# Merging an attention block and the routed experts behind it into one program, with eight expert blocks taken from early counts

## The chip, the cores and the metric

The kernel runs on one core of a Trainium2 chip. A core has a matrix engine (TensorE, PE in the profile, with its weight loads as PEld), a vector engine (DVE), an activation engine (ScalarE, ACT), a general engine (GpSimd, POOL) and a queue engine that issues transfers (SyncE, SP). Each engine takes its instructions in order, and they wait for each other by semaphores. The metric is the device time of one execution in microseconds (us); lower is better.

## The reference

Two layers run one after the other over x of 16 batches x 256 tokens x 128 features in float32. Each adds attention, normalises, adds a mixture of experts, and normalises again. The change lies in the first layer:

```python
# attention: 16 heads of 64, half-causal mask
scores = einsum('bhqd,bhkd->bhqk', q / sqrt(64), k);  attn = softmax(where(allowed, scores, -inf))
x = layernorm(x + (attn @ v) @ Wo)
# routed experts: 8 experts of 512, each token goes to its top two
topv, topi = top_k(x @ router_w.T + router_b, 2);  gates = softmax(topv)
for e in range(8):
    h = silu(x @ gate_w[e].T) * (x @ up_w[e].T)
    out += (h @ down_w[e].T) * sum(gates * (topi == e))
x = layernorm(x + out)
```

The second layer has a latent attention with rotary positions and another mixture of experts with two shared ones.

## The kernel before

The program is a sequence of stages: `attention0`, `routed0`, `attention1`, `routed1`, `final1`. The first two are the matter here.

`attention0` goes over 16 batches (numbered 0 to 15). A batch has eight pairs of heads and is worked in four periods (`period(i, u, batch)`, u from 0 to 3) of two pairs each. In a period TensorE makes scores, the value product of earlier pairs (`values`), the projections of the pair after next (`project_qk`, `project_v`) and transposes of probabilities (`turn`). DVE takes the maxima (`maxima`), ScalarE the exponentials (`exps`) and two kinds of copies out of PSUM (`turned`, `outputs`). The queue order of each engine is written out by hand in `period`; after period 3 of batch 15 comes a tail in which TensorE, ScalarE and DVE finish the last pairs. `project_v` may not start before `outputs` has freed its PSUM bank (`pe.wait_ge(ot_done, s - 2)`).

Tokens are routed as the batches go by. Period 1 makes the layernorm of the batch before (`residual`), period 3 its router, and period 0 of the next batch its choice of two experts: `choices` writes a one-hot tile, GpSimd keeps running counts per expert (`running_counts`), TensorE turns these into ranks (`ranks`), DVE into row numbers (`slots`), and GpSimd scatters each token's row into the memory region of its experts (`scatter_rows`, tensor xs). For the last batch all of this stands in the tail, one step behind the other, with nothing else left to do. When its choice is known, `tables` on DVE works out for each of at most 39 blocks of 256 rows which expert it belongs to (`expert`, `w_at`) and where its rows start (`in_at`).

Then the block of engine programs ends with a barrier, GpSimd clears the semaphores, and a second barrier follows (`nc.clear_and_free_semaphores`, `nc.all_engine_barrier`). `routed0` handles the 39 blocks. For each, SyncE loads its rows, TensorE transposes them (`turn_input`), ScalarE and DVE split inputs and weights into a high and a low part (`input_high`, `input_low`, `weights_high`, `weights_low`), TensorE makes gate and up products in two halves (`gate_up(j, u, 0)` and `(j, u, 1)`, 12 matmuls each) and the down product of the block before (`down`), ScalarE applies Silu (`gate`), DVE multiplies (`product`), ScalarE copies the result (`output`), and GpSimd scatters it with two indirect transfers (`scatter`, tensor yt). The first block runs with nothing before it to overlap with; the further ones run as a software pipeline, most of them in a hardware loop of eight blocks a turn. Behind `routed0` stands a barrier without a semaphore clear.

Of the kernel before, what the change touches and what calls it, by code (L numbers as in the profile page):

```python
# [21 lines left out]
P = 128  # L22
# [28 lines left out]
XW = P + 4  # L51
# [6 lines left out]
TAB = NB + 1  # L58
NB1 = 2 * NT // BR + E0 - 1
# [49 lines left out]
def attention0(nc, ctx, g, d):  # L109
# [4 lines left out]
    def sem(name):  # L114
# [44 lines left out]
    rk = sb("rk", [P, QB * 2, E0])  # L159
# [6 lines left out]
    before = sb("before", [P, P], F32R)  # L166
    S = g.psum[:, 0:4, :]
# [3 lines left out]
    VO = g.psum[:, 7, :]  # L171

# [14 lines left out]
    lg_ps, lg_done, oh_done, cum_done, rank_ps, rk_done, idx_done, count_ps = (sem(n) for n in (  # L187
        "lg_ps", "lg_done", "oh_done", "cum_done", "rank_ps", "rk_done", "idx_done", "count_ps"))
    zeroed, scattered, kept, pool_cum = sem("zeroed"), sem("scattered"), sem("kept"), sem("pool_cum")
    may_scatter, named = sem("may_scatter"), sem("named")  # L190
    rl_done, scaled = sem("rl_done"), sem("scaled")
    CONSTS = 4
# [7 lines left out]
    def after(eng, signal, n):  # L200

        if not isinstance(n, int) or n > 0:
            eng.wait_ge(signal, n)

    with nc.Block(no_gpsimd_drain=True) as block:
        @block.sync
        def _(sp):
# [45 lines left out]
            sp.wait_ge(w_in, 2 * B * 16)  # L253

        @block.scalar
        def _(act):
# [39 lines left out]
            def routed_columns(n):  # L296
                act.wait_ge(ntr_ps, n)
                nc.scalar.activation(halves(xr_h), TC, ACT.Copy).then_inc(nt_act, 1)
                nc.scalar.activation(halves(xr), TC, ACT.Copy).then_inc(nt_act, 1)

            def routed_ranks(n, bank=QK):
                act.wait_ge(rank_ps, n)
                nc.scalar.activation(rk[:], bank[:, 0:QB * 2 * E0].rearrange("p (g e) -> p g e", e=E0), ACT.Copy).then_inc(rk_done, 1)
# [8 lines left out]
            def period(i, u, batch):  # L312
# [15 lines left out]
                if u == 0 and batch > 1:  # L328
                    routed_ranks(i - 1)
# [3 lines left out]
                exps(s + 1, hp + 1, 1)  # L333

# [18 lines left out]
        def _(pool):  # L353
# [99 lines left out]
            scatter_rows(1, idx_last, nrm_last)  # L453
            pool.wait_ge(scattered, B * SCATTERS)

        @block.vector
        def _(dve):
# [104 lines left out]
            def slots(n, at=idx):  # L562
                dve.wait_ge(rk_done, n)
                chain.done(nc.vector.tensor_tensor(ohr[:], oh[:].bitcast(F32), rk[:], ALU.mult))
# [3 lines left out]
            def tables():  # L568
                t = g.t0

                wide = lambda a: a.unsqueeze(1).to_broadcast([P, TAB, E0])
# [2233 lines left out]
```

## Time and profile before

| | us |
|---|---|
| median of 3 runs | 1362.91 |
| lowest and highest run | 1362.71, 1364.22 |
| profiled execution, its own time | 1361.32 |
| its span, first to last instruction | 1359.5 |
| TensorE busy in the span | 1255.3 |
| DVE, ScalarE, GpSimd busy | 973.7, 922.3, 614.7 |

The views give, for the profiled execution, the instructions of each engine in order of time (timeline), their sum by source line (groups), and busy time, granted TensorE clock and transfers by stretch (windows). A clock of 1.00 is 2.4 GHz, 0.50 is 1.2 GHz. Matmuls overlap, and their ends are modelled, so a matmul that shows 0.28 us may be followed by the next after 0.12. The bracket behind a row of the timeline is the idle time of its engine before it and what ended that.

### The profile page before, as it was taken

How to read it: one execution, taken by the hardware profiler on the slowest of the kernel's cores; microseconds unless marked ns; L12 is line 12 of the kernel's file. 1: busy time of each engine (PE TensorE's matmuls, PEld its weight loads, DVE VectorE, ACT ScalarE, POOL GpSimd, SP SyncE). 2: the span in 40 equal slices, each digit the busy share in tenths (PEclk: the TensorE clock that was granted, in tenths of full speed). 3: DMA queues.
4: the chain of work that ended last, by engine and by line, in shares of the span. 5: the costliest groups of instructions: out<-in, count | busy, mean ns of one | idle time of the engine just before them, and what ended most of it. 6: DMA issues, size and time to landing. Idle time of an engine off the chain costs nothing. (4 is left out here: it accounts for less than half of the span.)

```text
span 1359.5 us, 34492 instructions
## 1 busy us (share of the span) xinstructions
PE 1255.3 (92%) x10782; PEld 1074.1 (79%) x10783; DVE 973.7 (72%) x2954; ACT 922.3 (68%) x2433; POOL 614.7 (45%) x967
## 2 busy tenths in 40 slices
PE   6999999999999999399999489999999999779996
PEld 5888888888888888399999467777777776558885
DVE  6788888877888876466666478899898987363443
ACT  4777777776677776265555357787878786657863
POOL 3244444444444444233333434465556552335773
PEclk9999999999999999599999769999999999989998
DMA  7021202020202020111111350222024200203326
GB/s 264 21 69 52 88 30 91 27 91 27 91 27 91 27 88 25 48 52 56 55 54 43 112 175 10 80 89 87 24 87 151 72 17 13 90 21 114 108 75 196
DMA packets 56445, 99.82 MB, mean 73 GB/s; under 512 B 11184, under 2 KB 46384, under 8 KB 53744
## 3 DMA queue, kind: packets, MB, share of 16 engines
q1 hardware_dynamic: 45840, 78.58, 18.2%
q0 software_dynamic: 9088, 18.89, 4.1%
q10 hardware_dynamic: 1440, 1.39, 0.3%
q8 instruction: 40, 0.66, 0.2%
q14 instruction: 37, 0.30, 0.1%
HBM read 77.85 MB, written 62.06 MB: 103 GB/s over the span
## 5 line engine op out<-in xcount | busy, mean ns | idle before, releaser
L271 ACT ACTIVATE a_prob<-psum,a_nmx 128x128 f32<-128x128 f32 (+1 forms) x512 | 208.2, 424 | 79.6 <-DVE a_nmx L496 79.6
L412 POOL TENSOR_TENSOR a_prob<-a_prob,a_rl 128x128 f32<-128x128 f32 (+1 forms) x256 | 124.4, 508 | 241.3 <-DVE a_rl L500 240.8
L2270 DVE TENSOR_REDUCE a_nmx<-psum 128x2 f32<-128x512 f32 x256 | 170.0, 685 | 22.5 <-PE psum L1555 19.4
L278 ACT ACTIVATE a_probt<-psum 128x768 f32<-128x768 f32 x128 | 105.1, 821 | 71.7 <-PE psum L716 71.7
L943 POOL DMA_INDIRECT yt<-m_yrow,m_dest x78 | 74.6, 957 | 129.2 <-ACT m_yrow L1018 117.4
L1927 ACT ACTIVATE a_prob<-psum 128x1024 f32<-128x1024 f32 x128 | 127.3, 1024 | 7.1 <-PE psum L1585 6.9
L1555 PE MATMUL psum<-k_stk,a_q_stk 96*128 96x256 f32 x512 | 117.2, 323 | 11.9 <-DVE a_nmx L2270 7.9
L1555 PEld LDWEIGHTS psum<-k_stk,a_q_stk 96*128 96x128 f32 x512 | 79.2, 197 | 42.8 <-issue 18.5
L716 PE MATMUL psum<-ident,a_prob 128*128 128x128 f32 x768 | 106.0, 274 | 1.7 <-ACT a_probt L278 1.0
L271 ACT ACTIVATION_READ_ACCUMULATOR a_prob<-psum,a_nmx 128x1 f32 x512 | 107.5, 210 | 0.0
L485 DVE TENSOR_TENSOR a_qkt<-psum,a_bqk 128x512 f32<-128x512 f32 x128 | 88.2, 689 | 22.0 <-PE psum L102 21.6
L1048 DVE TENSOR_TENSOR m_hid<-m_act_out,psum 128x512 f32<-128x512 f32 x78 | 53.6, 687 | 63.1 <-PE psum L102 46.2
L100 PE MATMUL psum<-m_x_h,m_w_h 128*128 128x256 f32 x312 | 95.3, 305 | 0.0
L1151 POOL DMA_INDIRECT yt<-m_yrow,m_dest x78 | 75.5, 968 | 41.9 <-DVE m_yrow L1298 21.3
L100 PE MATMUL psum<-a_xt_h,a_wqk_h 128*128 128x256 f32 x256 | 81.7, 319 | 8.5 <-DVE a_xt_l L481 7.1
L102 PE MATMUL psum<-m_x_l,m_w_h 128*128 128x256 f32 x312 | 89.1, 285 | 0.0
L101 PE MATMUL psum<-m_x_h,m_w_l 128*128 128x256 f32 x312 | 89.0, 285 | 0.0
L716 PEld LDWEIGHTS psum<-ident,a_prob 128*128 128x128 f32 x768 | 85.7, 141 | 2.3 <-issue 1.5
L496 DVE TENSOR_REDUCE a_nmx<-psum 128x2 f32<-128x512 f32 x128 | 87.0, 680 | 0.0
L1585 PE MATMUL psum<-a_q_stk,k_stk 128*128 128x256 f32 x512 | 85.4, 290 | 0.2 <-DVE a_o L2285 0.2
L1912 ACT ACTIVATE k_stk<-psum,a_in_head 96x256 fp32r<-96x256 f32 x192 | 74.5, 467 | 9.8 <-PE psum L1549 9.7
L2126 POOL DMA_INDIRECT xs<-a_nrm,a_idx x60 | 61.7, 1028 | 42.7 <-DVE a_idx L2356 27.3
(368 smaller groups left out, 3855.3 us busy)
## 6 DMA issues: line engine op xcount, KB each, us to landing
xs<-in_fill SPq DMA_DIRECT2D x144, 264.0 KB, 4.2
m_xrow<-xs SPq DMA_DIRECT2D x78, 132.0 KB, 2.1
w<-in_w SPq DMA_DIRECT2D x16, 256.0 KB, 3.4
a_yin<-yt SPq DMA_DIRECT2D x16, 256.0 KB, 2.7
f_yin<-yt SPq DMA_DIRECT2D x7, 512.0 KB, 8.0
w<-in_wr SPq DMA_DIRECT2D x2, 1284.0 KB, 7.8
yt<-m_yrow,m_dest POOLq DMA_INDIRECT x156, 2.2
xs<-in_fill_idle SPq DMA_DIRECT2D x2, 1056.0 KB, 6.6
```

The lines of the kernel that those rows point to most:

```text
L100: nc.tensor.matmul(out, wh, xh, start=start, stop=False)
L101: nc.tensor.matmul(out, wl, xh, start=False, stop=False)
L102: return nc.tensor.matmul(out, wh, xl, start=False, stop=stop)
L271: last = nc.scalar.activation(prob[:, hp % 4, h, at], S[:, 2 * (hp % 2) + h, at], ACT.Exp, bias=nmx[:, hp % 4, q, h:h + 1], accum_out=lsum ...
L278: nc.scalar.activation(probt[:, hp % 2], PT[:, :, 0:SW], ACT.Copy).then_inc(pt_done, 1)
L412: last = nc.gpsimd.tensor_tensor(prob[:, hp % 4, 0, at], prob[:, hp % 4, 0, at], rl[:, hp % 4, 0, q:q + 1].to_broadcast(prob[:, hp % 4, 0, ...
L485: nc.vector.tensor_tensor(qkt[:, hp % 2], QK.rearrange("p (j t) -> p j t", j=2), bqk[:, hp, :].unsqueeze(2).to_broadcast([P, 2, T]), ALU.a ...
L496: nc.vector.reduce_max(nmx[:, hp % 4, 1, :], two[:, :, P:SW], AX.X, negate=True).then_inc(nmx_done, 1)
L716: last = nc.tensor.transpose(PT[:, h, k * P:(k + 1) * P], prob[:, hp % 4, h, k * P:(k + 1) * P], g.ident[:])
L1555: last = nc.tensor.matmul(bank[:, q * T:(q + 1) * T], q_stk[0:KR, p, h // HG, q * P:(q + 1) * P], k_stk[p][0:KR, h, :], start=True, stop=True)
L1927: nc.scalar.activation(prob[:, k % 2, 2 * (t % 2):2 * (t % 2) + 2, :], ST[:, 2 * (t % 2):2 * (t % 2) + 2, :], ACT.Exp, scale=SCALE).then_i ...
L2270: nc.vector.reduce_max(nmx[:, :, h:h + 1], bank.rearrange("p (q k) -> p q k", q=QB), AX.X, negate=True).then_inc(mx_done, 1)
```

## The change

`attention0` and `routed0` become one function, `attention0_routed0`, in one block of engine programs with one set of semaphores. Of the 39 blocks, the first eight (`EARLY_BLOCKS`) are chosen differently: after 14 batches each expert has some full blocks of 256 rows, which later tokens can't change any more. The first eight of these are taken, in the order of the experts. Their table is worked out inside the last batch: `full_blocks` and `blocks_before` at the end of its period 0 on DVE, `early_experts` and `early_rows` at the end of period 1, `taken_blocks` at the end of period 2. The other 31 blocks get their table from the final counts less the blocks taken (`late_blocks`, `blocks_before`, `late_experts`, `late_rows`), in pieces between the products of blocks 2 to 4.

SyncE loads the rows of the eight blocks when the early table and the scatter of the fourteenth batch are there. ScalarE makes block 0's high weights at the end of period 2 of the last batch, after waits for the last weight load (`w_in`), the table and the last projection, and runs a one-column Silu behind the last exponential, so the table of that function is loaded there. The block steps of blocks 0 to 4 are written by hand between the steps of the last batch's output, layernorm, router and choice, on TensorE, ScalarE and DVE. The split weights, the Silu output and the block inputs use tiles and PSUM banks that attention has done with (`w_h, w_l = wqk_h, wqk_l`). The semaphore clear and the second barrier now come behind the experts. The core of the diff:

```diff
@@ SyncE
-            sp.wait_ge(w_in, 2 * B * 16)
+            sp.wait_ge(tabled, 1)
+            sp.wait_ge(scattered, (B - 2) * SCATTERS)
+            for j in range(SLOTS):
+                block_rows(j, j)
+            sp.wait_ge(tabled, 2)
+            sp.wait_ge(scattered, B * SCATTERS)
+            with sp.Fori(1, NB // SLOTS) as i:
...
@@ ScalarE, period and tail
+                if u == 2 and batch == B - 1:
+                    act.wait_ge(w_in, 2 * B * 16)
+                    act.wait_ge(tabled, 1)
+                    act.wait_ge(qk_ps, B * HP)
+                    block_weights_high(0, 0)
...
+            nc.scalar.activation(warm[:], bias[:, 0, 0:1], ACT.Silu)
             turned(B * HP - 3, HP - 3)
             outputs(B * PERIODS - 2, HP - 4)
             turned(B * HP - 2, HP - 2)
-            routed_ranks(B - 1, S[:, 2, :])
+            routed_ranks(B - 1, S[:, 1, :])
+            block_input_high(0, 0)
+            block_input_high(1, 1)
             turned(B * HP - 1, HP - 1)
+            block_gate(0, 0, 0)
+            block_weights_high(1, 1)
             outputs(B * PERIODS - 1, HP - 2)
-            routed_columns(B)
-            routed_ranks(B)
+            block_gate(0, 0, 1)
...
@@ DVE, period and tail
+                if u == 0 and batch == B - 1:
+                    full_blocks()
+                    blocks_before()
                 if u == 1 and batch > 0:
                     residual(i)
+                if u == 1 and batch == B - 1:
+                    early_experts()
+                    early_rows()
+                if u == 2 and batch == B - 1:
+                    taken_blocks()
...
             slots(B, idx_last)
-            tables()
+            late_blocks()
+            block_product(3, 3, 0)
+            blocks_before()
+            block_weights_low(4, 4)
+            block_product(3, 3, 1)
+            block_input_low(5, 5)
+            late_experts()
+            block_product(4, 4, 0)
+            late_rows()
+            block_weights_low(5, 5)
...
@@ GpSimd, behind the last scatter_rows
+            for j in range(SLOTS):
+                scatter_block(j, j)
+            with pool.Fori(1, NB // SLOTS) as i:
...
             pool.wait_ge(scattered, B * SCATTERS)
@@ program
-                attention0(nc, a, g, d)
+                attention0_routed0(nc, a, g, d)
             nc.clear_and_free_semaphores(g.sems)
             nc.all_engine_barrier(sem_only=True)
-            with ExitStack() as a:
-                routed0(nc, a, g, d)
```

How this moves instructions shows at two places. On TensorE, behind the transposes of the last batch's last but one pair (a_prob, L716), the kernel before has ranks, the last transposes, output products (a_wo) and the value product (a_v):

```order
547 L716 MATMUL psum<-ident,a_prob 128x128 x6
548 L759 MATMUL psum<-a_oh,a_before 128x32
549 L760 MATMUL psum<-cum,ones 128x32
550 L716 MATMUL psum<-ident,a_prob 128x128 x6
551 L744 MATMUL psum<-a_wo,a_ot 128x128 x4
```

In the new kernel the inputs of blocks 0 and 1 (a_xrow) are transposed before the last probabilities, and the first half of block 0's gate and up products (a_x_h with a_wqk_h, which now holds expert weights) comes before the output products:

```order
548 L961 MATMUL psum<-ident,a_prob 128x128 x6
549 L1004 MATMUL psum<-a_oh,a_before 128x32
550 L1005 MATMUL psum<-cum,ones 128x32
551 L1037 MATMUL psum<-ident,a_xrow 128x128 x2
552 L1146 MATMUL psum<-ident,a_xrow 128x128 x2
553 L961 MATMUL psum<-ident,a_prob 128x128 x6
554 L101 MATMUL psum<-a_x_h,a_wqk_h 128x256
555 L102 MATMUL psum<-a_x_h,a_wqk_l 128x256
556 L103 MATMUL psum<-a_x_l,a_wqk_h 128x256
```

So block work stands where TensorE went on with attention alone. On DVE, between periods 0 and 1 of the last batch, six instructions of the early table stand ahead of the maxima (a_nmx) of period 1, where the kernel before goes from the reciprocal straight to the maxima:

```order
303 L635 RECIPROCAL a_rl<-a_lsum 128x2
304 L720 SCALAR_TENSOR_TENSOR t_count<-a_rk,rc 128x8
305 L709 TENSOR_TENSOR t_more<-t_count,rc 128x128
306 L711 TENSOR_REDUCE t_blocks<-t_more 128x8
307 L714 TENSOR_TENSOR t_below<-t_blocks,rc 128x64
308 L716 TENSOR_REDUCE t_upto<-t_below 128x8
309 L717 TENSOR_TENSOR t_skip<-t_blocks,t_upto 128x8
310 L630 TENSOR_REDUCE a_nmx<-psum 128x2
```

And on DVE behind the last choice, where the kernel before ran its seventeen table instructions in a row, they now alternate with products (a_hid) and weight splits (a_wqk_l) of blocks 3 to 5:

```order
448 L754 TENSOR_REDUCE t_expert<-t_done 128x32
449 L755 TENSOR_SCALAR t_idle<-t_expert 128x32
450 L757 TENSOR_SCALAR t_w_at<-t_expert 128x32
451 L758 TENSOR_TENSOR t_done<-rc,t_expert 128x256
452 L773 TENSOR_TENSOR a_hid<-a_wv,psum 128x512
453 L762 TENSOR_TENSOR t_done<-t_done,t_start 128x256
454 L763 TENSOR_REDUCE t_at_start<-t_done 128x32
455 L764 SCALAR_TENSOR_TENSOR t_row<-rc,t_at_start 128x32
456 L765 TENSOR_TENSOR t_row<-t_row,t_idle 128x32
457 L766 TENSOR_SCALAR t_in_at<-t_row 128x32
```

The product of block 4 (452) has moved in among them.

## Rows read from the trace of the kernel before

**Rows 1.** Windows: stretch, length, busy PE, PEld, DVE, ACT, POOL, clock, DMA.
```profile
500.00:537.00 37.00, 36.07 (x352) 31.78 (x351) 29.25 (x107) 26.59 (x95) 17.01 (x34) 1.00 0.08 23
...
541.00:546.00 5.00, 4.05 (x38) 3.21 (x35) 0.25 (x2) 1.65 (x3) 2.04 (x2) 1.00 0.08 27
546.00:569.50 23.50, 3.87 (x15) 2.95 (x16) 10.45 (x45) 2.29 (x5) 8.49 (x14) 0.52 0.14 41
...
620.00:660.00 40.00, 40.00 (x347) 40.00 (x346) 25.24 (x41) 24.32 (x42) 15.89 (x17) 1.00 0.19 55
```

**Rows 2.** Timeline (start, us, engine, line), TensorE, end of last batch; brackets: idle before.
```profile
537.38 0.65 PE L727 MATMUL psum<-a_probt,a_v 128*64 128x256 f32 x4
...
540.70 0.85 PE L716 MATMUL psum<-ident,a_prob 128*128 128x128 f32 x6 [0.86 <-ACT a_probt L278]
...
544.83 1.16 PE L744 MATMUL psum<-a_wo,a_ot 128*128 128x128 f32 x8 [0.94 <-ACT a_ot L283]
```

**Rows 3.** Timeline, DVE, the tables behind the last choice.
```profile
556.36 0.16 DVE L573 TENSOR_TENSOR t_count<-psum,rc 128x8 f32<-128x8 f32 x1
...
557.71 0.17 DVE L580 TENSOR_TENSOR t_skip<-t_blocks,t_upto 128x8 f32<-128x8 f32 x1
557.79 0.48 DVE L581 TENSOR_TENSOR t_done<-t_upto,rc 128x320 f32<-128x320 f32 x1
...
561.13 0.18 DVE L593 TENSOR_SCALAR t_in_at<-t_row 128x40 int32<-128x40 f32 x1
```

**Rows 4.** Second barrier before the experts (one line's instructions), first expert matmul (timeline).
```profile
L2766 SPq EVENT_SEMAPHORE  x2: 17/17/17, 563.9 to 564.6; - x2
...
569.54 0.56 PE L100 MATMUL psum<-m_x_h,m_w_h 128*128 128x256 f32 x1
```

**Rows 5.** Timeline: block 1's first matmul, and two weight splits 35 blocks apart.
```profile
574.69 0.36 PE L100 MATMUL psum<-m_x_h,m_w_h 128*128 128x256 f32 x1
...
581.05 1.05 ACT L1014 ACTIVATE m_w_h<-w 128x1024 fp32r x1
...
751.54 1.05 ACT L1014 ACTIVATE m_w_h<-w 128x1024 fp32r x1
```

**Rows 6.** Groups in the loop, 580 to 740 us: count, busy us, mean ns, idle.
```profile
L943 POOL DMA_INDIRECT yt<-m_yrow,m_dest x66 | 63.2, 957 | 112.1 <-ACT m_yrow L1018 102.1 <-issue 10.1
...
L1048 DVE TENSOR_TENSOR m_hid<-m_act_out,psum 128x512 f32<-128x512 f32 x66 | 45.4, 688 | 52.1 <-PE psum L102 37.3 <-ACT m_act_out L1009 14.8
L1054 DVE TENSOR_TENSOR m_w_l<-w,m_w_h 128x1024 fp32r<-128x1024 f32 x33 | 40.4, 1225 | 7.4 <-ACT m_w_h L1014 7.0
```

**Rows 7.** Timeline, period 1 of the last batch: maxima, output copies, value projection.
```profile
512.34 0.42 DVE L495 TENSOR_REDUCE a_nmx<-psum 128x2 f32<-128x256 f32 x1 [0.21 <-PE psum L706]
...
514.99 0.85 ACT L283 ACTIVATE a_ot<-psum,a_bias 128x256 f32<-128x256 f32 x2
...
516.01 0.37 PE L100 MATMUL psum<-a_wv_h,a_xt_h 128*128 128x256 f32 x1
```

**Rows 8.** The same in period 2: output copies, value projection.
```profile
525.60 0.85 ACT L283 ACTIVATE a_ot<-psum,a_bias 128x256 f32<-128x256 f32 x2
...
526.72 0.36 PE L100 MATMUL psum<-a_wv_h,a_xt_h 128*128 128x256 f32 x1
```

**Rows 9.** Timeline, period 3: idle of DVE, ScalarE and TensorE.
```profile
530.04 0.42 DVE L495 TENSOR_REDUCE a_nmx<-psum 128x2 f32<-128x256 f32 x1 [0.86 <-PE psum L706]
...
531.09 0.37 ACT L271 ACTIVATE a_prob<-psum,a_nmx 128x128 f32<-128x128 f32 x1 [0.65 <-DVE a_nmx L496]
...
534.38 0.85 PE L716 MATMUL psum<-ident,a_prob 128*128 128x128 f32 x6 [0.73 <-DVE a_prob L506]
```

**Rows 10.** Timeline, ScalarE: the copy behind the last exponential; the table load in block 0.
```profile
535.67 0.87 ACT L278 ACTIVATE a_probt<-psum 128x768 f32<-128x768 f32 x1
...
571.41 1.28 ACT L1009 ACT_TABLE_LOAD   x1
572.70 0.60 ACT L1009 ACTIVATE m_act_out<-psum 128x512 f32<-128x512 f32 x1
```

More of the change, by code:

```diff
@@ L203, in after, with expert_offset @@
             eng.wait_ge(signal, n)
+    def expert_offset(engine, j):
+        at = w_at[0:1, bass.ds(j, 1)] if not isinstance(j, int) else w_at[0:1, j:j + 1]
+        return nc.values_load(at, engines=(engine,), min_val=0, max_val=(E0 - 1) * F0,
+                              skip_runtime_bounds_check_because="the table's rows are clamped")
     with nc.Block(no_gpsimd_drain=True) as block:
@@ new lines, in ranks, with block_gate_up @@
+                last.then_inc(rank_ps, 1)
+            def block_gate_up(j, u, a):
+                pe.wait_ge(xl_done, j + 1)
+                pe.wait_ge(wh_done, j + 1)
+                pe.wait_ge(wl_done, j + 1)
+                for out, before, base, signal in ((G, act_done, 0, gate_ps), (U, prod_done, F0, up_ps)):
+                    after(pe, before[a], j)
+                    for f in range(HB):
+                        c = slice(base + (a * HB + f) * P, base + (a * HB + f + 1) * P)
+                        last = split_mm(nc, out[:, a, f * BR:(f + 1) * BR], w_h[:, u % 2, c], w_l[:, u % 2, c], x_h[:, u % 2, :], x_l[:, u % 2, :],
+                                        True, True)
+                    last.then_inc(signal[a], 1)
@@ new lines, in block_down @@
+            def block_down(j, u):
+                w = expert_offset(mybir.EngineType.PE, j)
+                for a in range(2):
+                    pe.wait_ge(prod_done[a], j + 1)
+                after(pe, y_done, j - 1)
+                for h in range(2):
+                    for f in range(FB):
+                        last = nc.tensor.matmul(Y[:, u % 2, h * P:(h + 1) * P], hid[:, u % 2, f, h * P:(h + 1) * P],
+                                                g.wd[:, bass.ds(w + f * P, P)], start=f == 0, stop=f == FB - 1)
+                last.then_inc(down_ps, 1)
@@ L854, in _ @@
             pe.wait_ge(exp_done, B * HP * 2)
-            ranks(B - 1, S[:, 2, :])
+            ranks(B - 1, S[:, 1, :])
+            block_turn(0, 0, 16)
+            pe.wait_ge(row_in[1], 16)
+            for h in range(2):
+                last = nc.tensor.transpose(block_columns(1)[:, h * P:(h + 1) * P], xrow[:, 1, h, 0:P], g.ident[:])
+            last.then_inc(xb_ps, 1)
             turn(B * HP - 1, HP - 1)
+            block_gate_up(0, 0, 0)
             pe.wait_ge(ot_done, B * HP - 2)
@@ new lines, in _ @@
+            ranks(B, counts=True)
+            for j in range(3, SLOTS):
+                block_step(j, j, ((j + 2) // SLOTS + 1) * 16, False)
+            with pe.Fori(LOOPED_BLOCKS.start // SLOTS, LOOPED_BLOCKS.stop // SLOTS) as i:
+                for u in range(SLOTS):
+                    block_step(i * SLOTS + u, u, (i + (u + 2) // SLOTS) * 16 + 16, True)
+            for j in range(LOOPED_BLOCKS.stop, NB + 1):
+                block_step(j, j % SLOTS, ((j + 2) // SLOTS + 1) * 16, False)
```

463 lines of the change are left out of this document (247 added, 216 removed).

## The prediction

> **What bounds the kernel now.** I read the windows first [rows 1]: the busy time of each engine and TensorE's granted clock by stretch. The reader is to see three regimes. In attention (500 to 537 us) TensorE works 36.1 of 37 us at full clock, in the expert loop (620 to 660) 40.0 of 40.0. Between them, from 546 to 569.5, it works 3.9 of 23.5 us, and its clock falls to 0.52, near the lower of its two levels. That hole is what the change is about, so the second view is the timeline around it. TensorE ends its last big piece of attention [rows 2] with two waits of 0.86 and 0.94 us. Then one chain runs alone: layernorm of the last batch, router, choice, the tables on DVE, which end at 561.13 + 0.18 us [rows 3], the final scatter, a barrier, a semaphore clear and a second barrier (563.9 to 564.6), the first weight split and row loads, and the first expert matmul at 569.54 [rows 4]. Block 0 is then paid at the low clock: block 1 starts at 574.69, 5.15 us later, where a block costs 4.871 us in the loop ((751.54 - 581.05) / 35) [rows 5]. The end of the program stays as it is.
>
> **The anchor.** In the kernel before, block 5 starts at 574.69 + 4 x 4.871 = 594.17 us [rows 5]. From block 5 on both kernels run the same loop, 39 blocks in all, and TensorE sets its pace (no wait of TensorE in it, 100% busy) [rows 1]. So the gain is 594.17 minus the start of block 5 in the new kernel, minus what is added behind it. I work out that start on the clock of the trace before, with every delay added.
>
> **What TensorE has to do before it.** From 537.38, the value product of pairs 4 and 5 of the last batch's eight, to 545.99 it takes 8.61 us, of which 0.86 + 0.94 are waits and some 0.3 the modelled tails before them: 6.5 us of work [rows 2]. The new order puts between these pieces, and behind them, block work up to the second half of block 2's gate and up products: 2.7 blocks, 13.1 us at 4.871 [rows 5]. The transposes and the router of the last batch join at full clock; their matmuls are short, and I take 0.95 us for them (estimate: 8 matmuls at the loop's pace of about 0.12 us). Together 20.6 us.
>
> **Waits in that stretch.** First, the added Silu warm-up: behind its last exponential ScalarE copied the transposed probabilities from 535.67 to 536.54; a table load of 1.28 us and the one-column activation (0.2, estimate) now go ahead of the copy [rows 10], which ends near 538.0, so TensorE starts at 538.1, not 537.38: 0.7 us. Second, before the last transposes TensorE waited 0.86 us for ScalarE's copy; the rank matmuls and the transposes of blocks 0 and 1 fill it and about 0.7 is left, the copy itself being no faster. Third, block 0 needs ranks copied, both inputs copied (0.2 + 0.4), the slots and the low half on DVE (0.6 + 0.4) behind the rank matmuls, while TensorE has only the last transposes: 0.8 us. Sum 2.2 us. DVE then starts the second product of block 2 at 537.38 + 20.6 + 2.2 + 0.2 = 560.4 us.
>
> **From there DVE decides.** Its queue holds four products (0.688 each), two weight splits (1.225 each) [rows 6], two input parts (0.6 each, estimate: a steady block keeps DVE 3.1 us busy, 25.24 us in 8.2 blocks [rows 1], less two products and a split leaves 0.5), and in pieces the tables, which took 556.36 to 561.31 = 4.95 us before [rows 3], with the slots ahead of them, three small instructions of some 0.17: 5.5 us. The new tables have 32 entries, not 40, and one subtraction more: again about 5.4. Sum 2.75 + 2.45 + 1.1 + 5.4 = 11.7, and 0.6 for hand-offs: 12.3 us, so block 5's weights are ready at 572.7. TensorE alone would come there after a turn, the ranks and two blocks (10.3 us), so it waits about 2 us: the table work of 5.5 us, once all on the path, still costs 2.
>
> **What the change adds inside the last batch.** The three pieces of early table work stand at the ends of DVE's periods. (1) Six chained instructions behind period 0. The same six took 556.36 to 557.88 before, 1.5 us [rows 3]. DVE waited only 0.21 us there, then the maxima release ScalarE's exponentials, its two output copies end at 514.99 + 0.85 = 515.84, and TensorE's next value projection starts at 516.01, directly after them [rows 7]. No cover: 1.35 us. (2) Nine instructions behind period 1. The last eleven tables took 557.79 to 561.31 = 3.5 us with 40 entries [rows 3]; with 8, and two fewer, about 1.9 (five wide ones of 0.48 shrink to some 0.23: 320 elements take 0.48 and 8 take 0.17). The chain to TensorE is the same; the copies end at 526.45 and the projection starts at 526.72, behind two transposes [rows 8]. With 0.2 us of slack: 1.7 us. (3) Three behind period 2, 0.6 us, lie in an idle of 0.86 us [rows 9]: nothing. If that cover were gone, 0.6. (4) ScalarE's weight split of 1.05 us, which waits for the last weights and the early table, stands before period 3. ScalarE has 0.65 us of idle after it and TensorE has 0.73 us further on [rows 9]; about 0.45 us reaches the end. Sum of delays 1.35 + 1.7 + 0.45 = 3.5 us.
>
> The wait for the tables on the SyncE queue holds nothing but the row loads, whose slots are free; the eight early loads run where DMA is idle. GpSimd gets the final scatter of the rows ahead of the scatters of blocks 0 to 7, and is rid of that backlog since a block's two scatters cost 2 x (0.957 + 0.3) = 2.5 us against 4.87 [rows 6].
>
> **Behind the loop** the block's barrier is followed by the clear and the second barrier, which stood before the loop: 563.9 to 564.6 [rows 4]. 0.8 us are added there.
>
> **The sum.** Block 5 starts at 572.7 + 3.5 = 576.2 us. 594.2 - 576.2 = 18.0, less 0.8: 17.2 us. The profiled execution's span is 1359.5 us and its own time 1361.32; the median of the runs is 1362.91, 1.6 above it. I put the gain against the median: 1362.9 - 17.2 = 1345.7 us (span near 1342.3).
>
> **A rule weighed against the trace.** Of the table load the row shows 1.28 us, starting as the previous activation ends and followed directly by the Silu (571.41 to 572.70) [rows 10]. The Trainium skill, ScalarE: Activation LUTs, What ACT_TABLE_LOAD costs, states about 1.38 us of drain on top of 1.28. By that rule the sum would be 1.4 us less and the time 1347.1; the trace shows no drain.
>
> **Rivals.** *The small delays are absorbed.* TensorE's matmuls overlap, so its busy share in attention may hide room: weight loads fill 31.8 of 37 us there, and 40.0 of 40.0 in the loop [rows 1]. If the room lies where DVE's additions fall, the 3.05 us of (1) and (2) are free, and the time is 1342.6. For it: the difference of the two shares. Against: the projection that starts 0.17 us behind ScalarE's copy [rows 7]. The Trainium skill, Perfetto Trace Analysis, Identifying the Most-Contended Engine, judges TensorE by its weight loads rather than by matmul time; by that rule attention has headroom and this rival holds.
>
> *The interleaved stretch is looser than my sum.* Five blocks and the choice hand over about 30 times between TensorE, ScalarE and DVE; 0.1 us more at each is 3 us, and if the clock fell to its lower level in one of the waits, a block would cost 5.15 - 3.1 = 2 us more (gate and up halves, a turn) [rows 4, 5]. Time 1347.7 to 1350.7. Against it: with 4.05 of 5 us busy from 541 to 546 the clock stayed 1.00 [rows 1].
>
> *Slower than before:* GpSimd paces the loop. The rows of block 8 and later wait until the scatter of the block eight earlier has landed. If the two scatters of a block took more than 4.87 us instead of 2.5, every block from the eighth on would wait; at 5.5 us, 31 x 0.63 = 19.5 us are lost and the kernel is 2 us slower, 1365.2. For it: four row scatters are now queued ahead. Against: 66 of them took 957 ns each beside the same DVE load [rows 6].
>
> *It doesn't do what it says:* were the rows of the early blocks late (they wait for the scatter of the fourteenth batch and the table), block 0 would start where the kernel before has its barriers, and only these, the load behind them and the cold start were saved: (569.54 - 563.9) + 2 - 0.8 = 6.8 us, 1356.1 [rows 4]. Scatter and table are both issued by period 1 of the last batch, so little speaks for it.
>
> **How the numbers follow.** Forecast (12.5 to 19 us gained) 0.72; delays absorbed 0.12; looser 0.12; rows late 0.02; slower 0.02. Of the range's ends, the lower takes in the absorbed delays and 1 us of the wait of 2 at block 5 (1341.5), the upper the looser stretch up to its end (1350.5). A difference of 0.2% (2.7 us) is about what a measurement of this kernel can tell from no change. Faster by more 0.97, same 0.01, slower 0.02.
>
> **What would show it.** TensorE at clock 1.00 and without a wait over 2.5 us from 540 to block 5; the value projections of periods 1 and 2 of the last batch 1.35 and 1.7 us later against their predecessors; a TensorE wait of about 2 us before block 5, released by DVE's weight split; block period 4.87; the clear behind the loop. Wrong it would be made by a second hole in TensorE, a clock of 0.5 in it, or loop blocks longer than 4.9 us.

## The result, and the profile after

The changed kernel takes 1343.37 us (median of four runs, 1340.80 to 1343.72), the kernel before beside it 1362.81 (1361.02 to 1364.22). The ratio is 0.9862, with a 95% interval of 0.985 to 0.9875: 19.4 us are gained where 17.2 were forecast. The profiled execution took 1343.33 us, its span is 1341.5. One of the four runs of e3_early_moved below took 1993.29 us at a granted clock of 0.557 throughout; it is left out, and the median given there is that of the other three.

The windows of the changed kernel, three of the stretches of [rows 1], with the same columns:

```profile
500.00:537.00 37.00, 34.54 (x334) 29.74 (x332) 30.86 (x108) 24.57 (x88) 14.63 (x29) 1.00 0.18 53
...
546.00:569.50 23.50, 22.83 (x199) 22.04 (x198) 17.07 (x53) 12.67 (x25) 11.35 (x16) 1.00 0.06 19
620.00:660.00 40.00, 40.00 (x347) 40.00 (x346) 25.11 (x43) 24.34 (x42) 16.27 (x17) 1.00 0.19 55
```

The second row is the result. From 546 to 569.5 us TensorE is busy 22.8 of 23.5 us at full clock, where it was busy 3.87 us at 0.52. The loop (last row) is as before. In the first row TensorE has lost 1.5 of its 36.1 busy us: that is part of the price inside the last batch.

What TensorE still waits for, in the waits view of the changed kernel, 500 to 620 us (in all, times, longest):

```profile
PE psum L101 <- DVE a_wqk_l L779: 2.1, 2, 1.5
PE psum L922 <- DVE a_nrm L665: 1.2, 1, 1.2
PE psum L101 <- ACT a_ot L338: 1.1, 1, 1.1
PE psum L961 <- DVE a_prob L641: 1.0, 1, 1.0
PE psum L961 <- ACT a_probt L333: 0.4, 1, 0.4
```

In the kernel before, TensorE's first row in this view was 11.7 us for the rows of block 0. Now the longest is 1.5 us.

**A common clock for all runs.** Each execution comes to the last batch a little earlier or later, so I measure from one instruction, called A here: DVE's copy of queries and keys in period 0 of the last batch (before: 511.37; after: 511.73). In the timelines of DVE, before and after:

```profile
511.37 0.69 DVE L485 TENSOR_TENSOR a_qkt<-psum,a_bqk 128x512 f32<-128x512 f32 x1 [0.63 <-PE psum L102]
```

```profile
511.73 0.69 DVE L620 TENSOR_TENSOR a_qkt<-psum,a_bqk 128x512 f32<-128x512 f32 x1 [0.63 <-PE psum L103]
...
512.41 0.14 DVE L720 SCALAR_TENSOR_TENSOR t_count<-a_rk,rc 128x8 f32<-128x8 f32 x1
512.59 0.53 DVE L709 TENSOR_TENSOR t_more<-t_count,rc 128x128 f32<-128x128 f32 x1
...
513.99 0.17 DVE L717 TENSOR_TENSOR t_skip<-t_blocks,t_upto 128x8 f32<-128x8 f32 x1
514.19 0.42 DVE L630 TENSOR_REDUCE a_nmx<-psum 128x2 f32<-128x256 f32 x1
```

Ahead of the maxima (L630) now stand the six instructions of `full_blocks` and `blocks_before`, from t_count to t_skip. They delay the maxima from A + 0.97 to A + 2.46. On TensorE the marks are the output product in period 1, the scores of period 3 and the value product of pairs 4 and 5. Before (the last of these, 537.38, is in [rows 2]) and after:

```profile
517.52 3.73 PE L737 MATMUL psum<-a_wo,a_ot 128*128 128x128 f32 x32
...
528.96 0.49 PE L700 MATMUL psum<-a_qkt 64*128 64x128 f32 x4
```

```profile
517.74 0.38 PE L101 MATMUL psum<-a_wv_h,a_xt_h 128*128 128x256 f32 x1 [1.11 <-ACT a_ot L338]
...
519.27 0.49 PE L982 MATMUL psum<-a_wo,a_ot 128*128 128x128 f32 x3
```

```profile
532.28 0.49 PE L945 MATMUL psum<-a_qkt 64*128 64x128 f32 x4
...
540.94 0.65 PE L972 MATMUL psum<-a_probt,a_v 128*64 128x256 f32 x4
```

Less the 0.36 us between the two A, they are 1.39, 2.96 and 3.20 us later. The first matmul row also names the link: TensorE waited 1.11 us for ScalarE's output copy.

The stretch in which DVE decides, on DVE and then on TensorE (second product of block 2; weight splits and starts of blocks 4 and 5):

```profile
562.62 0.69 DVE L773 TENSOR_TENSOR a_hid<-a_wv,psum 128x512 f32<-128x512 f32 x1 [1.09 <-PE psum L103]
...
567.13 1.23 DVE L779 TENSOR_TENSOR a_wqk_l<-w,a_wqk_h 128x1024 fp32r<-128x1024 f32 x1 [0.62 <-DVE t_skip L717]
...
573.69 1.22 DVE L779 TENSOR_TENSOR a_wqk_l<-w,a_wqk_h 128x1024 fp32r<-128x1024 f32 x1 [0.60 <-DVE t_in_at L766]
```

```profile
568.62 0.36 PE L101 MATMUL psum<-a_x_h,a_wqk_h 128*128 128x256 f32 x1 [0.67 <-DVE a_wqk_l L779]
...
575.17 0.36 PE L101 MATMUL psum<-a_x_h,a_wqk_h 128*128 128x256 f32 x1 [1.46 <-DVE a_wqk_l L779]
```

Block 5 starts at 575.17 us, A + 63.44. In the kernel before it started at 594.18, A + 82.81. The gain at that point is 19.4 us, and it is still 19.4 us at the last scatter of the experts (A + 253.75 before, A + 234.37 after).

### The profile page after: what moved, and what is told of

The parts are those of the page before. It is cut to its first block and busy times, and to the rows that moved or that the text cites. A ratio compares the mean times of both kernels' runs of the same rounds, so it can differ in the third digit from the quotient of the medians.

```text
span 1341.5 us, 34497 instructions
## 1 busy us (share of the span) xinstructions
PE 1252.5 (93%) x10783; PEld 1070.9 (80%) x10784; DVE 976.9 (73%) x2973; ACT 921.5 (69%) x2434; POOL 618.2 (46%) x967
## 3 DMA queue, kind: packets, MB, share of 16 engines
q10 hardware_dynamic: 1440, 1.39, 0.3%
## 5 line engine op out<-in xcount | busy, mean ns | idle before, releaser
L577 POOL DMA_INDIRECT yt<-a_yrow,a_dest x78 | 75.2, 964 | 101.3 <-ACT a_yrow L373 87.1
L620 DVE TENSOR_TENSOR a_qkt<-psum,a_bqk 128x512 f32<-128x512 f32 x128 | 88.2, 689 | 21.7 <-PE psum L103 21.3
L773 DVE TENSOR_TENSOR a_hid<-a_wv,psum 128x512 f32<-128x512 f32 x78 | 53.6, 688 | 60.3 <-PE psum L103 44.5
L101 PE MATMUL psum<-a_x_h,a_wqk_h 128*128 128x256 f32 x312 | 94.3, 302 | 2.3 <-DVE a_wqk_l L779 2.1
L1254 POOL DMA_INDIRECT yt<-m_yrow,m_dest x78 | 75.5, 968 | 41.5 <-issue 21.2
L103 PE MATMUL psum<-a_x_l,a_wqk_h 128*128 128x256 f32 x312 | 88.1, 283 | 0.0
L102 PE MATMUL psum<-a_x_h,a_wqk_l 128*128 128x256 f32 x312 | 88.1, 282 | 0.0
```

The lines of the kernel that those rows point to most:

```text
L101: nc.tensor.matmul(out, wh, xh, start=start, stop=False)
L102: nc.tensor.matmul(out, wl, xh, start=False, stop=False)
L103: return nc.tensor.matmul(out, wh, xl, start=False, stop=stop)
L620: nc.vector.tensor_tensor(qkt[:, hp % 2], QK.rearrange("p (j t) -> p j t", j=2), bqk[:, hp, :].unsqueeze(2).to_broadcast([P, 2, T]), ALU.a ...
```

## The experiments

Nearly all edits move one or two microseconds of 1343, while the runs of one kernel differ by one to four. So for each run the table gives distances in its profile, in us: from A to the value product of pairs 4 and 5; from A to the last scatter of the experts (all that the change touches up to the barrier); from there to the next stage's first work, GpSimd's a_yw; and from there to the end of the span, which no edit touches.

| | A to values | A to last scatter | to a_yw | a_yw to end | median us |
|---|---|---|---|---|---|
| before | 126.01 | 253.75 | 6.89 | 587.5 | 1362.81 |
| after | 129.21 | 234.37 | 6.93 | 588.5 | 1343.37 |
| a0_changed | 129.24 | 234.43 | 7.13 | 590.0 | 1344.96 |
| e1_hoist | 129.23 | 233.61 | 7.11 | 588.0 | 1341.34 |
| e2_spread | 129.24 | 232.77 | 6.88 | 587.0 | 1341.11 |
| e3_early_moved | 126.46 | 231.72 | 7.22 | 590.8 | 1342.20 |
| e4_no_warmup | 129.24 | 234.30 | 7.02 | 589.9 | 1344.76 |
| e5_second_clear | 129.24 | 234.44 | 8.24 | 589.3 | 1344.77 |
| e6_not_interleaved | 129.22 | 247.70 | 7.01 | 587.1 | 1357.00 |
| e7_early_and_spread | 126.48 | 230.08 | 7.03 | 588.0 | 1338.56 |
| e8_both_again | 126.46 | 230.04 | 7.16 | 586.6 | 1337.73 |
| e9_tables_earlier | 126.47 | 229.76 | 7.19 | 589.0 | 1337.30 |
| e10_split0_later | 126.46 | 229.67 | 7.01 | 586.5 | 1337.54 |

The first two columns repeat within 0.07 us where the code ahead of the mark is the same. The fourth (a_yw to end) wanders between 586.5 and 590.8 whatever the edit, so a difference of one or two microseconds between two medians says little. a0_changed to e3 shared a chip, as did e4 to e7, and e8 to e10; the kernel before took 1361.65, 1361.90 and 1359.98 there.

**The changed kernel again.** 

> The changed kernel again, beside the next ones: 1343.4 us. Its profile should again show TensorE waiting 0.67 and 1.46 us for DVE's low weights of blocks 4 and 5, block 5 starting near 575.2 us, and the loop at 4.87 us a block.

Ratio 0.9882 (0.9866 to 0.9899). A to last scatter is as it was, 234.43.

**The register load ahead of the table pieces.**

```diff
             block_product(3, 3, 0)
+            w4 = expert_offset(mybir.EngineType.DVE, 4)
             blocks_before()
-            block_weights_low(4, 4)
+            block_weights_low(4, 4, w4)
...
             block_product(4, 4, 0)
+            w5 = expert_offset(mybir.EngineType.DVE, 5)
             late_rows()
-            block_weights_low(5, 5)
+            block_weights_low(5, 5, w5)
```

> DVE's register loads for the weights of blocks 4 and 5 stand behind a long product instead of behind a chain of table instructions; nothing else is changed. In the trace of the changed kernel DVE stands idle 0.62 and 0.60 us ahead of these two splits, both behind a chain, while a load behind a product shows no idle. Theory (DVE's queue decides when blocks 4 and 5 start): both idles go, block 5 starts 1.2 us earlier, time 1342.2. Rival (the load costs its 0.6 us wherever it stands): no change, and the idle shows up behind the product.

A to last scatter fell by 0.82 us, not 1.2. DVE's timeline around the two splits:

```profile
566.14 1.23 DVE L779 TENSOR_TENSOR a_wqk_l<-w,a_wqk_h 128x1024 fp32r<-128x1024 f32 x1
...
572.38 1.23 DVE L779 TENSOR_TENSOR a_wqk_l<-w,a_wqk_h 128x1024 fp32r<-128x1024 f32 x1 [0.25 <-DVE t_in_at L766]
```

The idle of 0.62 us is gone at block 4 and 0.25 of 0.60 is left at block 5. So a register load costs DVE time where it stands behind a chain, and next to none behind a long product: the rival falls, and DVE's queue does decide. The 0.25 us left is not the load's: in e2_spread a product with no register load before it stands idle 0.24 us behind the same t_in_at. The Trainium skill, DMA: Bandwidth & Descriptors, Latency and other measured facts, gives about 600 ns as the floor of a register load (`tensor_load`). The idle of 0.60 to 0.62 us has that size, but the records of the two loads themselves are shorter, 0.43 us at 566.6 and 0.30 us at 573.2. The median is 3.6 us below a0_changed, which is more than the edit did: 2 of them lie behind a_yw.

**The late tables behind the weight splits.**

```diff
-            late_blocks()
             block_product(3, 3, 0)
-            blocks_before()
             block_weights_low(4, 4)
+            late_blocks()
             block_product(3, 3, 1)
             block_input_low(5, 5)
-            late_experts()
+            blocks_before()
             block_product(4, 4, 0)
-            late_rows()
             block_weights_low(5, 5)
             block_product(4, 4, 1)
             block_input_low(6, 6)
+            late_experts()
...
+            block_weights_low(6, 6)
+            late_rows()
```

> The late tables are moved behind the weight splits: blocks after split 4 and before block 4's product, experts behind block 4, rows inside block 5. Theory: DVE's stretch of 12.3 us is what TensorE waits for (0.67 + 1.46 us), a block leaves DVE 4.87 - 3.1 = 1.8 us free, so the tables fit there and both waits go: 2.1 us faster, 1341.3, block 5 at 573.0. Rival 1 (TensorE's waits merely move to blocks 6 and 7): no gain, waits of 1 to 2 us there. Rival 2 (the rows of block 8 come late, since the late table is ready 3 to 4 us later): a wait for a row load before block 8, slower by up to 2 us.

It gained 1.66 us (234.43 to 232.77). Both waits for DVE's low weights went, no wait for rows came (rival 2 falls), and none at blocks 6 and 7 (rival 1). But a wait that nobody had named took 0.66 back, in TensorE's timeline, ahead of the down product of block 5. The view names nothing that ended it ("issue"); what it is comes out further down:

```profile
578.77 2.05 PE L1033 MATMUL psum<-wd,a_hid 128*128 x16 [0.66 <-issue]
```

**The early table work moved into DVE's idle time.**

```diff
-                if u == 0 and batch == B - 1:
+                if u == 1 and batch == B - 1:
                     full_blocks()
                     blocks_before()
+                    early_experts()
                 if u == 1 and batch > 0:
                     residual(i)
-                if u == 1 and batch == B - 1:
-                    early_experts()
-                    early_rows()
                 if u == 2 and batch == B - 1:
-                    taken_blocks()
+                    early_rows()
...
             block_weights_low(0, 0)
+            taken_blocks()
             slots(B - 1)
```

(The table signal is split in three, so that ScalarE waits for the experts and SyncE for the rows.)

> The early table work leaves the ends of DVE's periods 0, 1 and 2 of the last batch: full_blocks, blocks_before and early_experts (11 instructions, 2.6 us) stand ahead of the layernorm of period 1, where DVE waits 2.81 us for TensorE's output product; early_rows (0.85 us) at the end of period 2; taken_blocks in the tail behind the split of block 0's weights, where DVE waits 1.95 us. Theory (the predicted delays 1 and 2 are on the path, 1.39 and 1.57 us as the trace has them): 2.9 us faster, 1340.5, TensorE's value product of pairs 4 and 5 (540.94 us) at 538.0. Rival (the room is elsewhere and the delays are absorbed later, so they cost nothing at the end): no change in the start of block 5. Second rival (the layernorm now starts late behind 2.6 us of tables): only half of it gained.

A to values fell from 129.24 to 126.46, by 2.78, and A to last scatter from 234.43 to 231.72, by 2.71. What comes back in the batch is still there 230 us later. So the delays (1) and (2) lay fully on the path, and the rival of absorbed delays falls. Nor is the layernorm late: behind the eleven instructions DVE still waits 0.23 us for TensorE, and 0.45 us of delay remain (126.46 against 126.01), all but 0.08 of it from `early_rows`, which with 1.3 us is too long for the idle of 0.86 us [rows 9]. In DVE's timeline, the residual sum:

```profile
522.15 0.42 DVE L648 TENSOR_TENSOR a_res<-psum,a_xres 128x256 f32<-128x256 f32 x1 [0.23 <-PE psum L982]
```

**The Silu warm-up left out.**

```diff
-            nc.scalar.activation(warm[:], bias[:, 0, 0:1], ACT.Silu)
```

> The one-column Silu behind the last exponential is left out, so the table load comes later in ScalarE's queue, ahead of block 0's first Silu. The prediction charged the warm-up 0.7 us at the value product; the trace of the changed kernel shows no delay there. Theory from that trace: the warm-up cost nothing where it stood, and the load ahead of block 0's gate delays the gate by about 0.9 us, most of which the 1.5 us idle of ScalarE before the last output copies takes up: no change to 0.3 us slower, 1343.4 to 1343.7. By the prediction's term: 0.7 us gained at the value product. By the drain rule: a gap of 1.38 us ahead of the load at its new place.

A to last scatter is 234.30 against 234.44 in e5_second_clear on the same chip, and A to values is 129.24 in both: at most 0.1 us, where the prediction's term was 0.7. ScalarE's timeline with the warm-up (the changed kernel):

```profile
539.43 1.28 ACT L435 ACT_TABLE_LOAD   x1
540.72 0.20 ACT L435 ACTIVATE a_warm<-a_bias 128x1 f32<-128x1 f32 x1
540.83 0.79 ACT L333 ACTIVATE a_probt<-psum 128x768 f32<-128x768 f32 x1
542.60 0.84 ACT L338 ACTIVATE a_ot<-psum,a_bias 128x256 f32<-128x256 f32 x2 [0.97 <-PE psum L975]
```

and without it:

```profile
539.34 0.88 ACT L333 ACTIVATE a_probt<-psum 128x768 f32<-128x768 f32 x1
542.61 0.84 ACT L338 ACTIVATE a_ot<-psum,a_bias 128x256 f32<-128x256 f32 x2 [2.40 <-PE psum L974]
...
545.25 0.81 ACT L333 ACTIVATE a_probt<-psum 128x768 f32<-128x768 f32 x1 [0.39 <-PE psum L960]
546.08 1.28 ACT L364 ACT_TABLE_LOAD   x1
...
549.41 0.84 ACT L338 ACTIVATE a_ot<-psum,a_bias 128x256 f32<-128x256 f32 x2 [0.50 <-PE psum L974]
```

With it, the copy of the transposed probabilities moves from 539.34 to 540.83, but the output copy (L338) behind it does not move, as it waits for TensorE: the 2.40 us of idle shrink to 0.97. Without it the load falls into the idle ahead of the output copy at 549.41 (0.50 left of 1.53). At both places it is hidden. Nor does a drain show: with or without the warm-up the load starts directly as the instruction before it ends.

**A second clear and barrier.**

```diff
             nc.clear_and_free_semaphores(g.sems)
             nc.all_engine_barrier(sem_only=True)
+            again = [nc.alloc_semaphore(f"again{k}") for k in range(len(g.sems))]
+            nc.clear_and_free_semaphores(again)
+            nc.all_engine_barrier(sem_only=True)
```

> Behind the experts a second semaphore clear of as many semaphores and one more barrier are added: a dose of the term that the prediction put at 0.8 us. Theory A (a clear and a barrier are on the path): 0.9 us slower, 1344.3. Theory B (the first load of the next stage waits for something else, as the trace suggests: from the last expert scatter to the first combined rows it is 6.89 us in the kernel before and 6.93 us in the changed one, with the clear in it): no change.

From the last scatter to a_yw it took 8.24 us, 1.2 more than the mean of 7.06 of the eleven profiles with one clear. The median did not tell (1344.77 against 1344.76). Of that, 0.93 us lie ahead of the barrier's end (4.68 us behind the scatter, against 3.75 with one clear). So theory A holds for a clear that is added. The first clear, though, cost 0.04 in the profiled pair. GpSimd's timeline, last scatter, first work behind the barrier and a_yw; before and after (with the second clear they stand at 746.03, 750.71 and 754.27):

```profile
765.12 0.96 POOL L943 DMA_INDIRECT yt<-m_yrow,m_dest  x1 [0.31 <-issue]
767.93 0.10 POOL L2139 MEMSET a_one<- 128x1 f32 x1 [1.86 <-POOLq L918]
...
772.01 1.03 POOL L2088 TENSOR_TENSOR a_yw<-a_yin,a_pr 128x512 f32<-128x512 f32 x1 [2.66 <-DMA a_yin<-yt]
```

```profile
746.10 0.96 POOL L577 DMA_INDIRECT yt<-a_yrow,a_dest  x1 [0.30 <-issue]
749.85 0.10 POOL L2242 MEMSET a_one<- 128x1 f32 x1 [2.80 <-POOLq L2870]
...
753.03 1.03 POOL L2191 TENSOR_TENSOR a_yw<-a_yin,a_pr 128x512 f32<-128x512 f32 x1 [1.76 <-DMA a_yin<-yt]
```

The clear does put the barrier 0.94 us later (3.75 against 2.81 us behind the scatter), but from the barrier to a_yw it takes 3.18 instead of 4.08 us. SyncE issues the load of a_yin 0.02 us behind GpSimd's first instruction, not 0.34, and it is there 0.6 us sooner after the issue. In all twelve profiles with the clear this last stretch took 3.13 to 3.56 us, and 4.08 only in the one profile of the kernel before. Why it was slower there no run tells.

**One program, but nothing interleaved.** Block steps 0 to 4 stand behind the last batch's ranks on all three engines (shown for TensorE):

```diff
             ranks(B - 1, S[:, 1, :])
-            block_turn(0, 0, 16)
...
             turn(B * HP - 1, HP - 1)
-            block_gate_up(0, 0, 0)
             pe.wait_ge(ot_done, B * HP - 2)
             output_pairs(4, 6)
...
             pe.wait_ge(lg_done, B)
             ranks(B, counts=True)
+            block_turn(0, 0, 16)
...
+            block_gate_up(0, 0, 0)
+            pe.wait_ge(xl_done, 2)
+            block_gate_up(0, 0, 1)
```

> One part undone: one program and the early table stay, but the steps of blocks 0 to 4 come behind the last batch's ranks on TensorE, ScalarE and DVE instead of between its steps. The ranks ended at 555.4 us in the kernel before; with the added delays of 3.6 us they end near 559, block 0 starts at about 561 with TensorE at its lower clock, block 1 5.15 us later, blocks 2 to 5 at 4.87 each and 2 us of waits for the late tables: block 5 at 587.5, 12.3 us later than in the changed kernel, time 1355.7. Rival (what pays is only that barrier, clear and first loads are off the path, interleaving adds little): within 3 us of the changed kernel.

13.3 us later at the last scatter (247.70 against 234.44), 12.2 in the medians. The rival falls: interleaving gives 13.3 of the 19.4 us. The other 6.1 are what is left of the rest of the change, less the delays of 3.2 us inside the last batch: no barrier, clear or first load stands between choice and experts any more, and the tables are in pieces. Which part gives how much of them was not tried. Block 5 starts at 589.02 us. TensorE's windows (columns as in [rows 1]):

```profile
547.00:563.00 16.00, 6.92 (x42) 5.69 (x39) 5.59 (x29) 2.46 (x7) 6.80 (x13) 0.70 0.06 18
563.00:568.00 5.00, 5.00 (x29) 5.00 (x28) 2.47 (x4) 2.56 (x4) 3.63 (x4) 0.60 0.12 41
568.00:573.00 5.00, 5.00 (x45) 5.00 (x44) 3.19 (x7) 2.91 (x5) 0.96 (x1) 1.00 0.04 14
```

The hole is back (6.9 of 16 us busy), the granted clock falls to 0.70 and 0.60 on average over these stretches, and is full again only from 567 us, when block 0 is nearly through (the window from 566 to 567 us shows 0.50, the one from 567 to 568 shows 1.00).

**Both moves together.** The edits of e2_spread and e3_early_moved.

> The early table work moved into DVE's idle time and the late tables moved behind the weight splits, together. If both act on the same path one after the other, the gains add: 2.9 + 2.1 = 5.0 us, 1338.4. Rival: an earlier start leaves less cover in the interleaved stretch (the waits for ScalarE's copies grow), and only the larger of the two is seen, about 1340.5.

230.08 against 234.43: 4.35 us, and 2.71 + 1.66 = 4.37. The gains add. The ratio to the kernel before is 0.9828 (0.9812 to 0.9845). Repeated:

> The version with the early tables in DVE's idle time and the late tables behind the weight splits, again, beside the next two: 1338.6 us, TensorE waiting 0.7 us ahead of the down product of block 5 for nothing that the trace shows.

230.04, ratio 0.9831 (0.9818 to 0.9844).

**The tables one step earlier.**

```diff
             block_weights_low(5, 5)
+            late_experts()
             block_product(4, 4, 1)
             block_input_low(6, 6)
-            late_experts()
+            late_rows()
             block_product(5, 5, 0)
             block_weights_low(6, 6)
-            late_rows()
```

> The same version with late_experts directly behind block 5's weight split and late_rows before block 5's first product, so that the table signal and the row loads behind it come 3.4 us earlier (about 572.3 instead of 575.75 us). It asks what the wait of 0.7 us is that both versions with spread tables show ahead of the down product of block 5. If it goes with the table signal (SyncE's row loads start within 0.4 us of it), it moves 3.4 us earlier, to the down product of block 4, or goes. If it belongs to that place in TensorE's own instructions, it stays there. The time changes by at most 0.7 us: 1337.9 to 1338.6. If the products of blocks 4 and 5 now come late behind the tables, TensorE waits for DVE up to 0.5 us instead.

The wait of 0.68 us went, at the same place in TensorE's code. So it isn't that place. Nor do SyncE's row loads explain it: in e7_early_and_spread TensorE's register load for this down product ran at 574.6 and took its usual 0.30 us, 1.5 us before SyncE began its first (576.1). What the code says is that a down product waits for both products of its block (`pe.wait_ge(prod_done[a], j + 1)`), and late_rows had been moved right ahead of the second product of block 5. Here is that product in e7_early_and_spread on DVE, and the down product on TensorE:

```profile
576.01 0.69 DVE L774 TENSOR_TENSOR a_hid<-a_wv,psum 128x512 f32<-128x512 f32 x1 [0.26 <-DVE t_in_at L767]
```

```profile
576.90 1.38 PE L1033 MATMUL psum<-wd,a_hid 128*128 x10 [0.68 <-issue]
```

DVE's product ends at 576.70, and TensorE starts 0.20 us later. In e2_spread and e8_both_again the distance is the same (578.57 to 578.77, 577.27 to 577.46). In e9_tables_earlier late_rows stands one product earlier: the second product of block 5 ends at 575.22, and the down product starts at 576.38 without a wait. So the wait is one for DVE, which the view did not name: what rival 1 of e2_spread said of blocks 6 and 7 happened in a smaller size at block 5. A wait of 0.35 us for DVE's weights came in its place, so 0.3 us are gained (230.04 to 229.76). Ratio 0.9825 (0.9811 to 0.9838).

**Block 0's weight split behind the copy.**

```diff
-                if u == 2 and batch == B - 1:
-                    act.wait_ge(w_in, 2 * B * 16)
-                    act.wait_ge(tabled, 1)
-                    act.wait_ge(qk_ps, B * HP)
-                    block_weights_high(0, 0)
...
-            nc.scalar.activation(warm[:], bias[:, 0, 0:1], ACT.Silu)
             turned(B * HP - 3, HP - 3)
+            act.wait_ge(w_in, 2 * B * 16)
+            act.wait_ge(tabled, 1)
+            act.wait_ge(qk_ps, B * HP)
+            block_weights_high(0, 0)
```

> On top of the version before: ScalarE's split of block 0's high weights (1.05 us) moves from the end of period 2 of the last batch to behind the copy of the transposed probabilities, where ScalarE waits 0.97 us, and the Silu warm-up (1.4 us) is left out, which showed no effect by itself. The prediction put the split at 0.45 us, the trace of the changed kernel at 0.25. If that term is right, TensorE's value product of pairs 4 and 5 comes 0.25 to 0.45 us earlier against the start of the last batch, and the time is 0.3 us lower. Rival: the split now delays the output copy of the pairs before, and nothing is gained.

Nothing was gained: A to values is 126.46, against 126.47 with the split in period 2. ScalarE's timeline shows why. The first exponential of period 3, in e9_tables_earlier with the split ahead of it, in e10_split0_later without:

```profile
529.47 1.10 ACT L369 ACTIVATE a_wqk_h<-w 128x1024 fp32r x1
...
531.36 0.37 ACT L326 ACTIVATE a_prob<-psum,a_nmx 128x128 f32<-128x128 f32 x1
```

```profile
532.70 0.37 ACT L326 ACTIVATE a_prob<-psum,a_nmx 128x128 f32<-128x128 f32 x1 [1.02 <-DVE a_nmx L629]
```

They start at A + 120.18 and A + 120.17 (A is 511.18 and 512.53): DVE's maxima release them, and without the split ScalarE waits 1.02 us. So the split cost nothing at its old place, and my reading of 0.25 us for it was wrong too: in the changed kernel ScalarE also waits for the maxima behind the split (0.20 us, at 534.66). The three last versions are equal by their runs. They beat both kernels: 1337.3 to 1337.7 us, 22 to 23 below the kernel before on that chip.

## Why the prediction was right, point by point

The forecast was 1345.7 us in a range of 1341.5 to 1350.5; the time is 1343.37. All times of the trace after are less 0.36 us here, the distance of the two A.

*The delays inside the last batch.* (1) Forecast 1.35 us, measured 1.39. (2) Forecast 1.7, measured 2.96 - 1.39 = 1.57. (3) was to vanish in an idle of 0.86 us [rows 9] and cost 0.24: two of its three instructions took 0.40 and 0.54 us, so they lasted 1.19 us instead of 0.6. (4) Forecast 0.45, measured 0: once the maxima of period 3 are 3.20 us late, nothing behind them is later than that. Sum 3.20 against 3.5, and e3_early_moved gave 2.7 of it back.

```profile
532.60 0.40 DVE L742 SCALAR_TENSOR_TENSOR t_taken<-t_skip,t_taken 128x8 f32<-128x8 f32 x1
533.03 0.54 DVE L743 SCALAR_TENSOR_TENSOR t_first<-t_taken,rc 128x8 f32<-128x8 f32 x1
533.60 0.42 DVE L630 TENSOR_REDUCE a_nmx<-psum 128x2 f32<-128x256 f32 x1
```

*The waits of the stretch* were the step that failed most. The warm-up cost 0, not 0.7 (e4_no_warmup). The prediction let the value product of pairs 4 and 5 wait for the copy behind the table load; but the copy holds the second of the two pairs, whose part of the product starts at 541.68 us, 0.74 us behind the first, where before it was 0.70 (538.08 against 537.38). The rest of ScalarE's lateness ended in its own idle. The last transposes waited 0.36 us instead of 0.7. The third wait, 0.8 us ahead of block 0, isn't there either: block 0 starts at 545.32, where the transposes before it end (545.20). From the value product to the second product of block 2 it took 21.7 us where 22.3 were forecast. So the waits were 1.1 us shorter than forecast (0.36 against 1.5), and the work was 0.5 us longer (21.3 against 20.8): two errors that half cancel.

*DVE decides.* Forecast 12.3 us from that product to block 5's weights. Measured from 562.62 to 573.69 + 1.22 = 574.91: 12.3. The two waits for it, 0.67 + 1.46 = 2.1 us, were forecast as 2. Of DVE's 12.3 us, 1.2 are idle ahead of the two weight splits, where register loads stand behind chains, which the sum had only as 0.6 for all hand-offs; all else took 11.1 where 11.7 were forecast. That the two sums agree is luck by 0.6 us.

*Block 5* was forecast at 576.2 us and started at 574.8, the gain there 19.4 instead of 18.0: 0.7 from the warm-up, 0.6 from the stretch, 0.3 from the delays, less some 0.26 between the end of the split and the first matmul.

*Behind the loop* the term of 0.8 us was mis-sized: 0.04 in the profiled pair, 0 to 0.3 in the others. The barrier did come 0.94 us later, as the rows of the kernel before had it, but the prediction priced the barrier and not what stands behind it, the load of a_yin.

*The sum.* 19.37 - 0.04 = 19.3 against 17.2, and 19.4 by the runs. The spans differ by 18.0 only, since the untouched second layer took 1 us longer in the profile after.

*The rivals.* Delays absorbed: refuted by e3_early_moved, though the time alone (1343.4, near the rival's 1342.6) would have spoken for it. The Trainium skill's rule to judge TensorE by its weight loads (Perfetto Trace Analysis, Identifying the Most-Contended Engine) finds headroom in attention, 31.8 of 37 us; the runs show that this is no room for a delay in the chain from the maxima through ScalarE's copies to the projection. A looser stretch: five blocks ran at full clock with 2.5 us of waits. GpSimd as the pace: its scatters took 964 ns each, and between them it still waited for ScalarE's rows (19.6 us from 500 to 620 us). Rows late: the loads of the early blocks went out at 527 us, 16 us ahead of their first use.

## What to carry to other kernels

Price an added instruction by the chain that it stands in, not by the busy share of its engine: 3.6 us of small DVE work at the ends of two periods cost 3.0 us, and 2.6 us of it ahead of a wait of 2.8 us on the same engine cost nothing. When a copy or a table load is delayed, look up which product really needs it, and how long its engine will be idle before the next; here 1.4 us on ScalarE were free at two places. For an edit of one or two microseconds compare distances between two instructions of the trace that enclose the edit: they repeated within 0.07 us, while the rest of the program wandered by four. Where a view puts a wait down to nothing, read in the code what the instruction waits for, and look up when each of these ended: here that found a wait of 0.7 us for DVE.

## What the runs showed of the hardware

Some small DVE instructions take two or three times as long beside GpSimd. The comparison t_more with 128 elements took 0.53 us at 512.59 and 0.29 at 564.39; t_first took 0.54 us for 8 elements at 533.03, and 0.17 in e3_early_moved at 540.38. Both times that it was long a GpSimd product ran beside it, as in these timelines of GpSimd in the changed kernel, and of DVE in e3_early_moved:

```profile
512.57 1.02 POOL L530 TENSOR_TENSOR a_prob<-a_prob,a_rl 128x128 f32<-128x128 f32 x2 [3.18 <-DVE a_rl L635]
```

```profile
540.38 0.17 DVE L744 SCALAR_TENSOR_TENSOR t_first<-t_taken,rc 128x8 f32<-128x8 f32 x1
```

The Trainium skill, SBUF — State Buffer, SBUF: two separate sides, says that DVE and GpSimd share a pair of ports which one of them holds for its whole instruction, for a DVE operation with two inputs in SBUF; the rows of t_more and t_first agree. Others don't fit it so simply. In e7_early_and_spread t_in_at, with one input, took 0.47 us at such a moment too. In e3_early_moved t_row, with two inputs, took its usual 0.17 us at 530.45 beside a GpSimd product shown from 530.11 to 531.09, and t_more took 0.54 us at 519.37 beside a scatter. So when an instruction is held up stays open.

A semaphore clear takes 0.52 us on GpSimd with a drain of 0.19 ahead of it, and with its barrier 0.9 us from barrier to barrier:

```profile
L2869 POOLq DRAIN  x1: 194/194/194, 748.9 to 748.9; - x1
L2869 POOLq EVENT_SEMAPHORE_RANGE_CLEAR  x1: 523/523/523, 749.1 to 749.1; - x1
```
